# A fused two-block convolution kernel on one core: patches of 14 x 9 pixels in place of 14 x 8, 14 windows a unit in place of 17

## The reference, cut to what matters

```python
x = x + _L0_conv_ref(_gn(x), ...)   # dense products over rows and channels, with a gate
x = x + _L1_conv_ref(_gn(x), w_off, b_off, w_def)

# _L1_conv_ref: a deformable 3 x 3 convolution
x = relu(x)
offset = conv3x3(x, w_off) + b_off          # 18 channels: (dy, dx) for 9 taps
py, px = base_y + off[:, :, 0], base_x + off[:, :, 1]
samp = bilinear_gather(x, py, px)           # zero outside the image
out = einsum('bckhw,ock->bohw', samp, w_def)
```

## Time and profile before

| what | before |
|---|---|
| median of 3 runs | 1554.31 us (1554.22 to 1556.41) |
| the profiled execution | 1554.93 us, its span 1553.1 us |
| PE busy, share of the span | 1475.3 us, 95% |
| DVE, ACT, POOL busy | 1057.3, 1036.0, 1006.9 us (68, 67, 65%) |
| DMA engines of SP's queue, mean over 16 engines | 58.8% |
| moved by DMA | 268.12 MB |

### The profile page before, as it was taken

One profiled execution on the slowest core, in us unless ns is written; L12 is line 12 of the kernel. 1 busy time (PEld: TensorE's weight loads), 2 busy tenths in 40 slices (PEclk: granted clock), 3 DMA queues, 4 the chain that ended last, 5 costly groups with the idle time before them and its releaser, 6 DMA issues.

```text
span 1553.1 us, 28171 instructions
## 1 busy us (share of the span) xinstructions
PE 1475.3 (95%) x9363; PEld 987.8 (64%) x9364; DVE 1057.3 (68%) x2155; ACT 1036.0 (67%) x1884; POOL 1006.9 (65%) x627
## 2 busy tenths in 40 slices
PE   4999999964999999999999999999999999999997
PEld 3777777742566666666666666666666666666664
DVE  4988888863666666666666666666666666666664
ACT  2555555535777777777777777777777777777762
POOL 3555555634777667777776677777667777766671
PEclk9999999975999999999999999999999999999999
DMA  4333433334666666666666666666666676666660
GB/s 134 111 113 116 120 112 112 105 123 127 191 196 202 200 196 200 196 198 200 203 193 198 198 200 199 201 193 199 197 192 200 184 211 203 200 191 201 184 175 29
DMA packets 190711, 268.12 MB, mean 173 GB/s; under 512 B 19810, under 2 KB 128382, under 8 KB 190590
## 3 DMA queue, kind: packets, MB, share of 16 engines
q1 hardware_dynamic: 190590, 266.60, 58.8%
HBM read 188.33 MB, written 78.18 MB: 172 GB/s over the span
## 4 chain that ended last, share of the span: by engine, by line
PE 74%; SPq 1%; DMA 1%; POOL 1%; DVE 0%; ACT 0%; issue 0%; POOLq 0%; DVEq 0%
PE bank L854 33%; PE pair L822 24%; PE pair L870 7%; PE pair L899 7%; PE pair L837 2%; POOL weights L1681 1%; DMA hat_x<-hats 0%; SPq L628 0%; DMA hx_all<-hat_x 0%; SPq L611 0%; SPq L617 0%; ACT dist L1073 0%; SPq L632 0%; DVE hats L1377 0%; POOL offs_parts L1692 0%
## 5 line engine op out<-in xcount | busy, mean ns | idle before, releaser
L1681 POOL TENSOR_TENSOR weights<-hy_all,hx_all 112x768 f32<-112x768 f32 x384 | 746.9, 1979 | 324.8 <-PE bank L854 303.3
L1392 DVE SCALAR_TENSOR_TENSOR samples_lo<-bank,samples_hi 128x288 f16<-128x288 f32 (+1 forms) x1024 | 452.5, 462 | 356.9 <-ACT samples_hi L1080 351.3
L854 PE MATMUL bank<-weights,zT 112*128 112x288 f32 (+1 forms) x2176 | 597.0, 403 | 0.3 <-DVE samples_lo L1392 0.3
L1080 ACT ACTIVATE samples_hi<-bank 128x288 f16<-128x288 f32 (+1 forms) x1024 | 393.7, 418 | 205.6 <-PE bank L854 189.0
L854 PEld LDWEIGHTS bank<-weights,zT 112*128 112x128 f32 x2176 | 380.9, 190 | 132.0 <-DVE samples_lo L1392 28.9
L822 PE MATMUL pair<-samples_hi,w_hi 128*128 128x512 f16 x576 | 218.9, 380 | 1.3 <-DVE samples_lo L1392 1.3
L822 PE MATMUL pair<-samples_lo,w_hi 128*128 128x512 f16 x576 | 217.6, 378 | 0.0
L822 PE MATMUL pair<-samples_hi,w_lo 128*128 128x512 f16 x576 | 217.4, 377 | 0.0
L870 PE MATMUL pair<-ident,z 128*112 128x128 f32 x1088 | 172.3, 273 | 3.3 <-DVE zT L1412 2.6
L870 PEld LDWEIGHTS pair<-ident,z 128*112 128x112 f32 x1088 | 133.1, 134 | 59.3 <-DVE zT L1412 3.3
L1588 POOL TENSOR_TENSOR samples_lo<-samples_hi,samples_lo 128x512 f16<-128x512 f32 x64 | 74.2, 1159 | 126.1 <-ACT samples_lo L985 126.0
(11 more groups left out here) (142 smaller groups left out, 1774.1 us busy)
## 6 DMA issues: line engine op xcount, KB each, us to landing
hy_all<-hat_y SPq DMA_DIRECT2D x384, 192.0 KB
hx_all<-hat_x SPq DMA_DIRECT2D x384, 192.0 KB
hat_y<-hats SPq DMA_DIRECT2D x256, 126.0 KB
raw<-x_pad SPq DMA_DIRECT2D x68, 272.0 KB, 4.6
x_pad<-hy_all SPq DMA_DIRECT2D x64, 272.0 KB, 3.4
weights<-in_x SPq DMA_DIRECT2D x64, 256.0 KB, 3.0
out<-y SPq DMA_DIRECT2D x32, 512.0 KB, 3.6
hat_x<-hats SPq DMA_DIRECT2D x128, 72.0 KB
```

The source lines that it names most:

```text
L854: mm = nc.tensor.matmul(sampled_step(n, p)[:, :, c0 - first:c1 - first], zT[0:WPIX, u * WINDOWS + w, :], weights[0:WPIX, u, :, c0:c1], sta ...
L1080: nc.scalar.activation(samples_hi[:, u, :, c0:c1], sampled_step(n, p), ACT.Copy).then_inc(samples_ready, 1)
L1392: nc.vector.scalar_tensor_tensor(out=samples_lo[:, u, :, c0:c1], in0=sampled_step(n, p), scalar=1.0, in1=samples_hi[:, u, :, c0:c1], op0=A ...
L1681: nc.gpsimd.tensor_tensor(to, hy_all[0:WPIX, i * TROWS:(i + 1) * TROWS, :], hx_all[0:WPIX, i * TROWS:(i + 1) * TROWS, :], ALU.mult).then_i ...
```

## The change

A window is five columns of samples wide in place of four, so its patch is 14 x 9 pixels, 126 in place of 112. A unit then has 14 windows and 13 steps in place of 17 and 16; the window of a full step is 360 elements wide in place of 288, and the last step is 20 + 4 columns in place of 16 + 8. The table of steps is written for 13 steps and four groups of turned windows. Since 9 is not even, the y hats are stored three times in place of two, and each is repeated three times by the spread in place of four. Everything that hangs on `SRC_C` follows: the x hats have 81 rows, a piece fills 72 partitions, a padded row has 138 columns in place of 136.

```diff
-BR, WC, UW = 8, 4, 64
+BR, WC, UW = 8, 5, 64
...
-COPIES = 2
+COPIES = 3
...
-            "h0 s0 s1 s2 k0 h1 c0 c1 s3 s4 T0 k1 z0 z1 O0 s5 P0 s6 r0 k2 c2 c3 s7 s8 T1 c4 k3 c5 s9 s10 "
-            "k4 c6 T2 s11 s12 c7 k5 p0 T3 s13 s14 Q0 c8 G0 T4 s15 R0").split()]
+            "h0 s0 s1 s2 k0 h1 c0 c1 s3 s4 T0 k1 z0 z1 O0 s5 P0 r0 k2 c2 c3 s6 s7 T1 c4 k3 c5 s8 "
+            "k4 c6 T2 s9 c7 k5 p0 T3 s10 s11 Q0 c8 G0 s12 R0").split()]
...
-                if p == STEPS - 1:
-                    pe.wait_ge(zT_a, zT_copied(n, TGROUPS - 1)[0])
...
-                    wait(pe, zT_a, zT_copied(n, 0)[0] - 1)
+                    wait(pe, zT_v, zT_copied(n, 0)[1])
```

## The result

| what | before | after |
|---|---|---|
| median of 4 runs | 1554.26 us (1554.08 to 1556.41) | 1648.01 us (1645.27 to 1652.03) |
| ratio, 95% interval | | 1.0602 (1.058 to 1.0624) |
| the profiled execution, its span | 1554.93, 1553.1 us | 1645.35, 1643.5 us |
| moved by DMA | 268.12 MB | 305.15 MB |

The change costs 93.8 us, 6.0%.

The account below looks back on a forecast made before the run. PE bounds the kernel before; after the change SP's DMA loop was to. First loop to 374 us, 62 loops of 20.5 us to 1645, 59.6 us to the end less 1, 1.8 outside the span: 1705 us, range 1,630 to 1,790.

Parts of the forecast that it names:

- SP's loop becomes the bound through the eight common engines: SP's DMA loop in stage 2: packets on engines every DMA starts with make it 20.5 us, above PE's 17.8.
- The sign against it, a share well above 0.55 in a backlog: DMA share in a backlog: well above 0.55 would mean the common eight engines are not the bound.
- The loop, 20.5 us: SP's loop per unit after the change: 18.3 us of packets, 1.7 quiet, 0.5 for y and pixels.
- The 3.2 us on top and the quiet 1.7: SP's loop: 3.2 us of starts, slow first packets and hindrance beyond priced packets; 1.7 us with no packet running.
- The surcharge of 0.5 us for y and pixels: SP's loop: y and two pixel blocks every second unit add 1.1 us there, 0.5 a unit.
- Larger spreads are issued as fast as smaller ones: SP's issue of a unit's twelve spreads: left at 7.9 us after the change.
- PE: 0.35 us a unit, 22 us: PE, three turns fewer a unit: unit 17.8 us in place of 18.15; alone 64 x 0.35 = 22 us gained.
- Where the stall goes: PE waits 2 to 3 us a unit before L837 or the first step, as late pieces delay POOL and `low_offsets`.
- POOL's 126 partitions: POOL's six products on 126 partitions against 112: no change from 11.73 us; upper bound 12.5%, 1.5 us.
- The clock falls: Rival: PE's clock drops in each stall; at 22.8 us a unit, 1,848 us; chance of over 1,790 us 0.07.
- The loop is barely over: Rival: half the extra 3.2 us goes as fewer engines run beside the eight; loop 18.9 us, 1,606 us; chance 0.06.
- PE stays the bound: Rival: SP's loop ends under PE's 17.8 us, so the kernel gets faster, 1,532 us; chance 0.08.

Follow-up runs that it names:

- e1: The changed kernel, but every spread moves only the first half of each row, 1,536 bytes in place of 3,072: 1547.62 us, 0.9952 of the kernel before.
- e2: The changed kernel, but all twelve spreads read 16 rows of y hats five times, over 16 engines, with 11% more bytes: 1548.08 us, 0.9957 of the kernel before.
- e4: The changed kernel with y hats stored once in place of three times, the y spread over 8 engines: 1633.89 us, 1.0511 of the kernel before.
- e8: The kernel before the change with a third store of the y hats that nothing reads: 1559.16 us, 1.0031.
- e11: The changed kernel with all spreads over 16 engines and only half of each row moved: 1547.21 us, 0.9949 of the kernel before.
- e5: The changed kernel with the next unit's stores put between the third and fourth pair of spreads in SP's loop: 1940.56 us, 1.2471 of the kernel before.
- e7: The changed kernel with three more 32-byte DMAs a unit on SP, among the spreads: 1684.17 us, 1.0823 of the kernel before.

## Why the prediction was right, and by how much it was off

The direction, the place and the mechanism held: 1648 us lies in the range of 1630 to 1790, near its lower end and 57 us under the forecast.

- **SP's loop becomes the bound through the eight common engines.** Shown: e1 shortens the packets, e2 spreads them evenly, and the loss is gone; e4 takes issue time away and it stays; e8 adds the stores without the larger spreads and has 0.3%. The 222 small packets came out to the piece, so the y spread does take 12 engines. The sign against it, a share well above 0.55 in a backlog, was badly set: where spreads alone run (1014 to 1020) the share is 0.69, since the other four engines of the y spread run beside the common eight; it doesn't tell which of them are full. The 0.56 of the drain is 9 of 16 engines, as 27 rows of x hats take by the prediction's pattern.
- **The loop, 20.5 us: mis-sized.** This is the term that made the error: it measured 19.52, and 62 x 0.98 = 61 us. The rest of the sum stood: second unit's stores at 375.3 (374 forecast), from the last stores to the end 1643.5 - 1585.3 = 58.2 us (58.6). Within the loop two errors ran against each other. From the stores' issue to the first spread it takes 3.8 us, where 20.5 - 6.6 - 7.9 = 6.0 was implied. The issue of the spreads takes 9.04 us, where I had left it at 7.9. By its DMA terms: in 28 loops without y from the middle (19.4 us on average) packets run for 17.5 us, where 18.3 was taken (14.9 + 3.2 is 18.1, not 18.2), and nothing runs for 1.9, where 1.7 was taken.
- **The 3.2 us on top and the quiet 1.7.** They were read from one start-up loop. The changed kernel's own start-up loop (387.45 to 408.13) takes 20.7 us against 20.0 forecast without y, so the carried-over price fits that place; but over stage 2 the loops run from 17.8 to 21.8 us, and the start-up is at their slow end: one engine works alone there from 406.6 to 407.8. Nor is the 3.2 mainly starts. Between 500 and 1450 us a packet of 3,072 bytes takes 0.174 us on average before and 0.157 after, one of 1,024 bytes 0.054 and 0.051. With these a common engine carries 72 x 0.174 + 48 x 0.054 = 15.1 us before and 90 x 0.157 + 72 x 0.051 = 17.8 after, where 11.5 and 14.9 were counted: the time on top sits in the packets, and it shrank per packet. The surcharge of 0.5 us for y and pixels measured 0.1: units behind whose stores they stand take 19.54 us, the others 19.43, since y and pixels run where the others have their quiet 1.9 us.
- **Larger spreads are issued as fast as smaller ones: wrong.** A y spread takes 0.75 us of SP's time in place of 0.57, 0.65 in e4 (8 engines) and 0.59 in e2 (16). That it goes by the count of engines fits these three rows, with 12 the dearest; shape and count change together here, so the cause isn't separated.
- **PE: 0.35 us a unit, 22 us: mis-sized.** e11 shows 0.25 us a unit, and a collision of DVE and POOL, which the trace of before doesn't have, takes more than half of that back in the profiled execution. Turns and full steps cost what I took; the steps behind the narrow last one did not.
- **Where the stall goes.** Right: in front of L837, behind `low_offsets`. It is 59.4 us in 51 units, 1.2 us each and not 2 to 3, since the loop is 1.6 us above PE's 17.9 and not 2.7. SP's wait for hats is gone, as forecast.
- **POOL's 126 partitions** cost nothing: six products in 11.63 us, 11.73 before.
- **The rivals.** *The clock falls*: in a few units, not in each stall. Five of the 45 waits in front of L837, of 2.2 to 3.8 us, are followed by a stretch at the lower of the two levels (1.2 GHz); behind the others, those of about 2 us too, PE stays at 2.4 GHz. One of the five, and the stretch behind it:

```profile
971.25 0.62 PE L837 MATMUL pair<-offs_parts,select 122*128 122x512 f16 x2 [2.88 <-POOL offs_parts L1690]
972.40:975.60 3.20, 3.20 (x8) 2.08 (x7) 2.32 (x5) 1.98 (x3) 0.00 (x0) 0.50 0.62 193
```

  Over the middle 1000 us that makes 0.99. In e5, where PE waits 178.7 / 41 = 4.4 us a unit, the clock is 0.92, and after one of 4.49 us the two locating products take 1.03 us as in the earlier trace rows: the rival's price is real where stalls are as long as in e5. *The loop is barely over*: its reason, less hindrance, is borne out in part by the shorter packets; that it is for fewer engines isn't shown (last section), and 19.5 lies between its 18.9 and my 20.5. *PE stays the bound*: e11 is that case, made by hand, and gains 8 us in place of 22.

The Trainium skill, "DMA: Bandwidth & Descriptors", section "Why a DMA increments its semaphore by 16 and not by 1", gave 12 engines for the y spread; the 20 small packets a pair agree. For the pile on the common engines e2 against the changed kernel gives 1648.0 - 1548.1 = 100 us, its shorter issue included. In e7 a third of an added issue time told, in e4 next to nothing of a saved one; a third of 1.35 us in 62 loops is 28 us, so the pile alone is worth an estimated 72 to 100 us.

## What to carry to other kernels

Read a DMA bound by engine, not by the mean share: count the small packets of each kind of DMA, lay them on the engines, and ask which engines are never idle; here a source with 16 rows outermost was worth 11% more bytes (e2). Price a closed loop from as many of its turns as the trace has; one turn at the start was its slow end here. Before a store is moved forward in a queue, follow what its wait would hold back: here (e5) it closed a chain through all five.

## What the runs showed of the hardware

**A packet of 3,072 bytes takes a different time in each kernel.** In 500 to 1450 us, the queue's row (packets, MB, share) of the kernel before, the changed one, e2 and e4, in this order:

```profile
q1 hardware_dynamic: 96908, 186.30, 67.6%
```

```profile
q1 hardware_dynamic: 108595, 202.49, 67.2%
```

```profile
q1 hardware_dynamic: 125883, 233.24, 92.4%
```

```profile
q1 hardware_dynamic: 80269, 177.64, 55.0%
```

MB over share x 16 x 950 us is the rate of a busy engine: 18.1, 19.8, 16.6 and 21.2 GB/s, against 24.4 with eight alone. The mean lengths of the 3,072-byte packets there have the same order: 0.174, 0.157, 0.204 and 0.139 us. So has the count of engines that the two spreads of a pair take (16 + 8, 12 + 8, 16 + 16, 8 + 8), but that more engines at work at once make a packet longer isn't shown: in the kernel before it takes 0.146 us with about 8 packets under way and 0.185 with 13 or 14, in the changed one 0.158 and 0.148. What lengthens it was not tried.

**A matrix product of 72 float32 columns** is as short as its share of a 360-column one in e11 (0.06 us from start to start), but the two products behind the pair come 0.05 us late each, and the weight loads there start 0.11 us apart. That the loads hold the products up is read from these starts; no run changes it.

**DVE's hats and POOL's product exclude each other for a whole instruction.** In e11 the hats take 0.68 or 2.33 us by which of the two engines began 0.03 to 0.08 us earlier; in all eight late units it was POOL. The Trainium skill, "SBUF — State Buffer", section "Who interferes with whom", says that DVE in a two-port mode, which a `tensor_scalar` can enter, contends with POOL for a shared pair of ports, and that whoever issues first has the pair for the whole instruction. The rows agree: the delay, 1.65 us, is nearly the product that began first (1.82 us in the trace). In the kernel before the hats start 0.15 us ahead (1000.99 against 1001.14) and take 0.683 us on average over 55 units.
